# A four-layer graph network on one core: the sync engine fetches five gathered tiles per layer row by row

## What is computed

```python
L0: segment_sum(support[src_all], dst_all) / cnt + b            # support = h @ weight
L1: lap = segment_sum(h[src] * edge_weight, dst)
    out = leaky_relu((h + lap) @ W1 + b1 + (h * lap) @ W2 + b2); out / norm(out)
L2: segment_sum(hn[src] * ef(edge_attr), dst), then two linear maps   # ef: two softplus layers on 100,000 edges
L3: attention with 4 heads: segment softmax over dst of leaky_relu(a_src[src] + a_dst[dst]),
    weighted segment_sum of h[src], mean of the heads, layernorm, relu
```

## Time and profile before

| | us |
|---|---|
| median of 3 runs | 4295.27 |
| the three runs | 4294.87 to 4297.35 |
| the profiled execution | 4303.76 |
| its span, from first to last instruction | 4302.4 |

### The profile page before, as it was taken

How to read it: one execution, slowest core, us unless ns; L and a number is a source line. 1 busy time by engine, 2 the same in 40 slices (tenths; PEclk the granted TensorE clock), 3 DMA queues, 4 the chain that set the end, 5 groups by cost and what they waited for, 6 DMA issues and landing times. The chain is left out here.

```text
span 4302.4 us, 57236 instructions
## 1 busy us (share of the span) xinstructions
PE 2439.7 (57%) x13354; PEld 2005.6 (47%) x13354; DVE 2591.9 (60%) x7217; ACT 1825.7 (42%) x4203; POOL 3069.9 (71%) x3240
## 2 busy tenths in 40 slices
PE   2666666654565656566444444444566665666667
PEld 1555545454444444455444434433445454455556
DVE  4444444443566666667443434443358999999998
ACT  3344444421244444432211111111257878778775
POOL 3777777776777777777577777777646777777764
PEclk8787787876777777778665665566678999999888
DMA  4444444432343443332233333333248222222221
GB/s 129 117 113 121 122 119 116 122 82 64 92 118 115 115 118 112 117 101 70 74 107 102 107 107 106 102 107 107 80 83 141 56 56 56 56 56 56 56 49 31
DMA packets 226492, 403.82 MB, mean 94 GB/s; under 512 B 59290, under 2 KB 124783, under 8 KB 226160
## 3 DMA queue, kind: packets, MB, share of 16 engines
q0 software_dynamic: 100608, 208.65, 19.7%
q10 hardware_dynamic: 65776, 121.56, 9.9%
q1 hardware_dynamic: 59784, 69.94, 5.3%
HBM read 332.15 MB, written 67.78 MB: 93 GB/s over the span
## 5 line engine op out<-in xcount | busy, mean ns | idle before, releaser
L671 POOL DMA_INDIRECT t_work<-d_T,t_tabG x3136 | 2968.5, 947 | 1079.7 <-issue 941.3
L1136 DVE TENSOR_TENSOR t_acc<-t_acc,ps 128x128 f32 (+1 forms) x732 | 210.7, 288 | 769.2 <-PE ps L555 473.3
L1079 PE MATMUL ps<-t_work,t_acc 128*128 x2592 | 421.7, 324 | 250.2 <-SPq L698 225.6
L1079 PEld LDWEIGHTS ps<-t_work,t_acc 128*128 128x128 f32 x2592 | 392.8, 235 | 315.3 <-issue 315.0
L1125 DVE TENSOR_TENSOR t_acc<-t_work,ps 128x512 f32<-128x512 f32 x244 | 167.2, 685 | 561.5 <-ACT ps L1204 561.5
L555 PE MATMUL ps<-t_acc,t_wts 128*128 128x512 f32 x392 | 316.3, 954 | 331.8 <-DVE t_acc L594 331.8
L1204 ACT COPY ps<-t_acc 128x512 f32 x244 | 140.4, 588 | 849.3 <-SPq L698 846.6
L1079 PE MATMUL ps<-t_acc 128*128 128x128 f32 x1296 | 286.4, 410 | 377.4 <-DVE t_acc L1125 377.3
L1079 PEld LDWEIGHTS ps<-t_acc 128*128 128x128 f32 x1296 | 264.5, 311 | 398.7 <-DVE t_acc L1125 398.7
L1609 PE MATMUL ps<-t_work,t_hT 128*128 x1960 | 322.1, 314 | 98.8 <-DVE t_acc L1619 83.2
L1609 PEld LDWEIGHTS ps<-t_work,t_hT 128*128 128x128 f32 x1960 | 271.6, 214 | 159.1 <-issue 159.0
(11 more groups left out here) (190 smaller groups left out, 4647.9 us busy)
## 6 DMA issues: line engine op xcount, KB each, us to landing
t_work<-d_T,t_tabG POOLq DMA_INDIRECT x3136
d_edge_net<-t_acc ACTq DMA_DIRECT2D x98, 512.0 KB
t_acc<-d_edge_net SPq DMA_DIRECT2D x98, 512.0 KB, 3.8
t_acc<-in_edge_attrT ACTq DMA_DIRECT2D x96, 512.0 KB
t_acc<-d_T ACTq DMA_DIRECT2D x12, 790.1 KB, 16.9
d_T<-t_acc ACTq DMA_DIRECT2D x22, 256.0 KB, 2.4
t_acc<-d_T SPq DMA_DIRECT2D x4, 790.1 KB, 14.9
d_T<-t_acc SPq DMA_DIRECT2D x10, 266.0 KB, 3.1
```

The source lines that it names most:

```text
L671: pool.indirect_dma_start(out=work[:, at:at + width], out_offset=None, in_=table, in_offset=bass.IndirectOffsetOnAxis(ap=idx[:, g * QUAD + ...
L1079: last = pe.matmul(sums(layer, s, width), masks[s % MASKS][:, k, :], rows_k, start=(k == 0), stop=(k == QUAD - 1))
L1136: dve.tensor_tensor(out=o, in0=o, in1=sums(layer, s, width), op=ALU.add).then_inc(e_acc[layer], 1)
```

## The change

In each layer, five of the 784 tiles are no longer gathered by POOL. They are the last tiles of the groups 42, 74, 106, 138 and 170 (`SIDE_AT`). SP fetches their rows one by one: for each row it loads the source index from `idx` into a register and issues one DMA of one row of the table into a side tile (a stretch of `acc` in layers 0 to 2, of `work` in layer 3; two stretches in turn). In each of the turns 0 to 159 SP does this for four rows (`SIDE_PER`), between `ready(n + 3)` and its wait for `used`. So 32 turns fill one side tile. When the ring's place for the group is free, in turn 34, 66, 98, 130 and 162, SP waits until the 128 rows have landed and copies the side tile into the ring with one DMA. `ready` of such a group waits for three gathers and for this copy.

```diff
+SIDE, SIDE_PER = 5, 4
+SIDE_BEGIN = [-(-(P * j) // SIDE_PER) for j in range(SIDE + 1)]
+SIDE_AT = [SIDE_BEGIN[j + 1] + RING + 2 for j in range(SIDE)]
...
                 pool.sem_inc(s_go, 1)
-                for k in range(QUAD):
+                for k in range(QUAD - (g in SIDE_AT)):
                     at = (g % RING * QUAD + k) * pitch
                     pool.indirect_dma_start(
...
+        s_placed = sem("s_placed")
+        s_row = [[sem(f"s_row{layer}{k}") for k in range(4)] for layer in range(4)]
+
+        def side_rows(layer, j):
+
+            lo, width = (MLP + 11 * GRP, ACC3) if layer < 3 else (0, ROW3)
+            return (acc if layer < 3 else work[:, RING * QUAD * ROW3:])[:, lo + j % 2 * width:lo + (j % 2 + 1) * width]
...
+        def fetch_rows(layer, table, n):
+
+            width = table.shape[1]
+            for j in range(SIDE):
+                at = QUAD * SIDE_AT[j] + QUAD - 1
+                for p in range(max(SIDE_PER * (n - SIDE_BEGIN[j]), 0), min(SIDE_PER * (n + 1 - SIDE_BEGIN[j]), P)):
+                    row, = numbers(ENG.SP, idx[p:p + 1, at:at + 1], 1, 0, N - 1)
+                    sp.dma_start(side_rows(layer, j)[p:p + 1, 0:width], table[bass.ds(row, 1), :])\
+                        .then_inc(s_row[layer][j % 4], 16)
+
+        def place_rows(layer, table, pitch, j):
+
+            width, at = table.shape[1], (SIDE_AT[j] % RING * QUAD + QUAD - 1) * pitch
+            sp.wait_ge(s_row[layer][j % 4], 16 * P * (j // 4 + 1))
+            sp.dma_start(work[:, at:at + width], side_rows(layer, j)[:, 0:width])\
+                .then_inc(s_placed, 16)
+
+        def gathered_by(n):
+
+            return sum(16 * (QUAD - (m in SIDE_AT)) for m in range(n % RING, n + 1, RING))
+
+        def relay_groups(layer, table, pitch):
...
-                sp.wait_ge(GATHERED[n % RING], landed[n % RING] + per * (n // RING + 1))
+                sp.wait_ge(GATHERED[n % RING], landed[n % RING] + gathered_by(n))
+                if n in SIDE_AT:
+                    sp.wait_ge(s_placed, 16 * (SIDE * layer + SIDE_AT.index(n) + 1))
                 sp.sem_inc(e_rdy[layer], QUAD)
...
                     ready(n + ahead)
                 if n + RING >= GROUPS:
                     continue
+                fetch_rows(layer, table, n)
                 sp.wait_ge(used, ends[n % 4])
                 sp.sem_inc(e_free[layer], 1)
+                if n + RING in SIDE_AT:
+                    place_rows(layer, table, pitch, SIDE_AT.index(n + RING))
                 if layer == 2 and n % 2 == 1:
                     load_net(n + RING - 1)
             for q in range(RING):
-                landed[q] += per * len(range(q, GROUPS, RING))
+                landed[q] += gathered_by(range(q, GROUPS, RING)[-1])
```

More of the change, by code:

```diff
@@ L37 @@
 assert STEPS % 2 == 0
+assert SIDE_AT[-1] < GROUPS
 assert GROUPS % 4 == 0 and 4 * HALFNET < STEPS
@@ L679, in gather_groups @@
                         gather_rows(2 * (g - RING + CB // 2) + c)
-        def relay_groups(layer):
-            per = 4 * 16
+        s_placed = sem("s_placed")
[3 more added lines that the diff above has]
+            return (acc if layer < 3 else work[:, RING * QUAD * ROW3:])[:, lo + j % 2 * width:lo + (j % 2 + 1) * width]
+        assert MLP + 11 * GRP + 2 * ACC3 <= BB * ACC3 and (RING * QUAD + 2) * ROW3 <= work.shape[1]
+        def fetch_rows(layer, table, n):
[14 more added lines that the diff above has]
+        def relay_groups(layer, table, pitch):
             used, closed_at, top_at = ((e_mm[0], closing2, PAIRED), (e_mm[1], closing2, PAIRED), (e_mul, closing, STEPS),
@@ L1228, in edge_loop @@
                 cleared.append(clear_sums(layer))
-            relay_groups(layer)
+            relay_groups(layer, table, ACC3)
             sum_groups(layer, width)
@@ L1692, in tensor_slot @@
                 turn_scores(q + 5)
-        relay_groups(3)
+        relay_groups(3, T3, ROW3)
         for q in range(-6, QUADSB):
```

## The result

The changed kernel took 4275.62 us, median of 5 runs (4273.73 to 4279.49), against 4295.37 us (4294.87 to 4300.0, 5 runs) of the kernel before: 19.75 us less, ratio 0.9953 with a 95% interval of 0.9938 to 0.9967, which is 14 to 27 us. The forecast was 4275.3 us. The profiled execution spans 4278.2 us, 24.2 us less than before.

A forecast was written before the change was run, and what follows sets the result against it. POOL's issue of indirect DMAs, 1.25 us apart, was taken to bound layers 0, 2 and 3. Saving 18.75 us there plus 1.25 in layer 1, with SP's rows hidden, gave 4295.27 - 20.0 = 4275.3 us; range 4268 to 4320.

The forecast's parts named there:

- The bound and the worth of a tile: POOL's gather issue bounds layers 0, 2 and 3; five gathers fewer save 6.25 us in each, 18.75 us together.
- Layer 1: DVE and PE pace its network phase, so only group 170's tile counts: 1.25 us, bounds 0 and 6.25.
- The rows' cost on SP: Load 0.30, arithmetic 0.15, issue 0.33, gaps 0.07: 0.85 us a row, hidden in SP's waits below 5.0 us a turn.
- My sign that SP would still wait in nearly every turn: SP at L698 still waits for landings in nearly every turn; waits vanishing in turns 0 to 159 would speak against the forecast.
- The Trainium skill's floor for a register load: About 600 ns per SP load would make a row 1.15 us, a turn 4.8, and layer 2 alone lose its gain.
- What queues behind the rows: Rows before SP's freeing of a ring place delay it 3.4 us, within the slack, and delay no consumer: cost 0.
- The slack of 17 us: How much later SP may free a ring place: about 17.3 us in layers 0 to 2, 7.3 in layer 3.
- one delay of 3.4 us: At the end of layer 1's network phase, if SP's wait for PE no longer covers the rows.
- The rival on SP: Four rows a turn make SP the bound from 1.20 us a row (1.13 in layer 2): slower, chance 0.21.
- My 5.2 and 5.5 us a turn: Example SP turn lengths for the rival on SP: 5.2 us gives 4403 us in all, 5.5 us gives 4595.
- One sign was ill chosen: L671 <- L714, SP's freeing releasing POOL, appearing in layer 0 or 2 would mean a turn's rows exceed 5.0 us.

The follow-up runs named there:

- the base: The kernel before with one register operation more (& 1023) in front of each wait on a loaded number; 4298.41 us, ratio 1.000 to the kernel before.

## Why the prediction was right

**The bound and the worth of a tile.** Right. 5 x 1.25 us came out as 6.1, 6.2 and 6.5 us in layers 0, 2 and 3 at equal pace, and as 13.7, 13.6 and 11.5 us with eleven tiles. Layer 3's consumers had the room that the earlier trace rows showed. That the median came within 0.3 us of the forecast is luck: the interval runs from 14 to 27 us, and the second time the change was run it gave 21.5 us.

**Layer 1.** Right in kind: 2.4 us instead of 1.25, and 2.8 where SP does nothing. That one of five tiles counts was read from the earlier trace rows. The term was a little small: the consumers don't keep POOL back in every period, so an earlier tile keeps a part of its worth. That is an argument; the runs show only the 0.6 to 2.9 us.

**The rows' cost on SP.** The sum of 0.85 us was 0.97 at the medians and 1.03 on average in layers 0 and 1, and its terms were wrong in opposite directions. The load takes 0.51 instead of 0.30. The number taken from the earlier trace rows was that of loads which follow a wait; here most loads stand right behind the issue of a row, and even the closing load of four numbers went from 0.297 to 0.468 when the rows came before it. It is not the issue of a DMA as such. In layer 2 the closing load stands right behind the 512 KB issue of L690 (L724 after), before and after:

```profile
L632 SPq TENSOR_LOAD <-t_closing x47: 294/302/309, 2125.1 to 3046.3; - x47
```

```profile
L636 SPq TENSOR_LOAD <-t_closing x47: 296/747/756, 2116.1 to 3029.3; - x47
```

Only with rows ahead of both does it take longer. What it is in them that does it, no run tells. The issue takes 0.255 instead of 0.33, and the arithmetic with the move 0.07 and its gaps instead of 0.15. For a whole turn I had 3.6 us (3.9 in layer 2), and SP was busy for 4.5 in layers 0 to 2. My sign that SP would still wait in nearly every turn missed: in the 131 turns between 200 and 850 us of layer 0 it waited 48 times. None of this reached the time, since 4.5 us is below 5.0, but the room was 0.5 us and not 1.4.

**The Trainium skill's floor for a register load**, "DMA: Bandwidth & Descriptors", section "Latency and other measured facts", about 600 ns: no row here bears it out as a floor, with 0.273 as the shortest of 2560 loads and 0.509 as their median; but for a load behind the issue of a row it came nearer than my 0.30.

**What queues behind the rows.** Right for four rows: neither leaving the rows out nor moving them behind the freeing changed the time beyond what can be measured. The slack of 17 us in layers 0 and 2 fits the freeing that could be 3.9 us later without one wait over 0.3 us. That the rows delay no consumer held as long as SP waits for landings. At the end of layer 1's network phase it does not, and with eight rows a turn the end of the layer came 14 us later; I had allowed one delay of 3.4 us there.

**The rival on SP.** It was right as a mechanism: at four rows, 4.5 us a turn, there is no loss, at five rows, 5.2 to 5.65 us, there is. But I read the margin as wider than it is; the change stood one row a turn from a loss of 268 us. My 5.2 and 5.5 us a turn gave 108 and 300 us.

**One sign was ill chosen.** I had said that a freeing as POOL's releaser in layer 0 or 2 would prove me wrong. It appeared 32 and 11 times, each with 0.3 us. The longest wait, not the name of the releaser, is what tells.

## What to carry to other kernels

When one engine issues at a constant pace and sets the time, each instruction taken off it is worth its pace, but only in the stretches where nothing else paces the ring: read that layer by layer from who waits for whom. The engine that takes the work over is free up to its idle time per turn and a cliff beyond it, so price its turn with the loads and issues as they will follow each other, and look at the stretched ones, not at the median alone. How much is left is read from its own waits in the stretch with the extra work, not from those of the whole layer. Ask also which of its signals stand behind the new work, and who needs them in a hurry. Where a per-item register load is the largest part of that turn, load several numbers at once: that doubled the work SP could take and brought 37 us instead of 20.

## What the runs showed of the hardware

- A register load of four numbers on SP took 0.30 us in the kernel before, behind a wait and right behind the issue of a 512 KB transfer alike. Right behind the issue of a row whose address comes from a register, one number took 0.51 us. As the first load of a turn, with `ready` between it and the rows, it took 0.44 us for one number, 0.47 for four and 0.70 for eight: from one to four numbers adds little, the next four add 0.23.
- Single loads take up to 2.7 us. In the changed kernel layers 0 and 1, beside which the edge network runs, have all of the long ones: the longest load of a row was 2.24 and 2.01 us there, 0.72 and 0.70 in layers 2 and 3. Layer 2 has 512 KB transfers as well, so these alone are not the cause, which stays open.
- A one-row DMA whose address comes from a register costs SP 0.255 us to issue, or 0.225 where no load stands between two of them, and one operation (0.037) and one move (0.029) for the address.
- The pace of POOL's indirect DMAs differs between profiled executions: in layer 2 it was 1.2483 or 1.2484 us in most, 1.2490 in one, and 1.2508 to 1.2511 in three, where the median gather took 0.947 instead of 0.944 (so it did with five rows a turn). It makes 8 us in 3136 gathers. Each kernel has one profile, but the medians of the kernel before and of the base agree (4298.49 and 4298.41) while their profiles have 0.947 and 0.944, which speaks for the execution rather than the kernel. Three of the four with 0.947 are of the session in which the kernel before was slowest (4302.08 us, against 4298.49 and 4295.58), and a fourth profile of that session has 0.944. What sets it I don't know; a comparison of two single profiles of this kernel can be off by that much.
